# A full float32 product for probabilities times v, in place of three split ones

## The reference

```python
q = rmsnorm(ln(x) @ wq.T, q_norm_w); k = rmsnorm(ln(x) @ wk.T, k_norm_w)   # 16 heads of 128
v = ln(x) @ wv.T
q, k = apply_rope(q), apply_rope(k)
scores = 50 * tanh(q @ k.T * 128 ** -0.5 / 50)        # causal mask, then softmax
x = x + (softmax(scores) @ v) @ wo.T                  # stage 1, attention
x = x + wkv(w, u, ln(x), ctx)                         # stage 2, a recurrence over the 128 positions
x = x + moe(ln(x)) + shared_ffn(ln(x))                # stage 3, 16 experts, top 6, and a shared one
```

## Time and profile before

| | |
|---|---|
| timed runs | 2131.62 us median of 3, 2123.41 to 2139.04 |
| the profiled execution: span from first to last instruction | 2047.4 us |
| its own device time | not given; the median of the timed runs is 84.2 us over the span |
| PE matmul busy | 1982.2 us, 97% of the span |
| PE weight load, DVE, ACT, POOL busy | 87%, 54%, 45%, 50% |
| mean granted clock of PE | 0.990 |

### The profile page before, as it was taken

The page is one execution under the profiler, slowest core; times in us unless marked ns, Lnnn a source line. Parts: engine busy times, 40 slices in busy tenths (PEclk is TensorE's granted clock), DMA queues, the critical chain, the costliest instruction groups (busy, mean ns, idle before and its releaser), DMA issues.

```text
span 2047.4 us, 40563 instructions
## 1 busy us (share of the span) xinstructions
PE 1982.2 (97%) x12012; PEld 1790.4 (87%) x12013; DVE 1112.9 (54%) x2413; ACT 917.8 (45%) x2119; POOL 1013.5 (50%) x1076
## 2 busy tenths in 40 slices
PE   6999999999999999999989999999999999999998
PEld 5788888888888888888878898899999999999997
DVE  4776666666677776777667555333333333333332
ACT  4555555554566666656555312233333333323332
POOL 5444444442344444544556206676733333588885
PEclk8999999999999999999989999999999999999999
DMA  8677777778877878788534238666633443499899
GB/s 321 199 240 257 254 255 253 256 254 279 295 256 282 322 252 304 279 280 288 199 117 167 93 104 284 210 217 216 229 122 121 123 129 123 143 214 218 193 213 242
DMA packets 188986, 450.47 MB, mean 220 GB/s; under 512 B 21696, under 2 KB 21952, under 8 KB 188864
## 3 DMA queue, kind: packets, MB, share of 16 engines
q1 hardware_dynamic: 135392, 338.68, 49.1%
q0 software_dynamic: 21504, 51.13, 10.6%
q10 hardware_dynamic: 31968, 59.12, 9.0%
HBM read 275.36 MB, written 173.48 MB: 219 GB/s over the span
## 4 chain that ended last, share of the span: by engine, by line
PE 84%; DVE 4%; DMA 3%; ACT 3%; POOL 2%; issue 2%; SPq 1%; ACTq 0%; POOLq 0%; DVEq 0%
PE bank L1139 21%; PE bank L979 15%; PE bank L1149 12%; PE bank L1030 7%; PE bank L1004 7%; PE bank L165 6%; PE bank L582 4%; PE bank L1016 3%; PE bank L592 3%; PE bank L599 2%; PE bank L1051 2%; PE bank L1063 1%; DMA xT<-xT_att 1%; DMA raw<-in_weights 1%; PE bank L1041 1%
## 5 line engine op out<-in xcount | busy, mean ns | idle before, releaser
L1139 PE MATMUL bank<-w_hi,xT 128*128 x1776 | 473.7, 329 | 2.3 <-DVE xT L1734 2.1
L979 PE MATMUL bank<-w_hi,xT 128*128 128x512 f32 x1024 | 356.3, 409 | 6.2 <-issue 3.3
L609 DVE TENSOR_TENSOR hT<-bank,hT 128x384 fp32r<-128x384 f32 x143 | 79.7, 557 | 472.5 <-ACT hT L606 472.5
L1139 PEld LDWEIGHTS bank<-w_hi,xT 128*128 128x128 f32 x1776 | 315.7, 188 | 10.3 <-issue 5.1
L1422 POOL TENSOR_TENSOR rr<-rr,expo 128x4 f32<-128x4 f32 x128 | 129.0, 1008 | 365.8 <-DVE rr L1620 365.8
L1139 PE MATMUL bank<-w_lo,xT 128*128 x888 | 286.3, 322 | 0.0
L979 PEld LDWEIGHTS bank<-w_hi,xT 128*128 128x128 f32 x1024 | 196.5, 192 | 47.3 <-issue 6.6
L1149 PE MATMUL bank<-w_hi,hT 128*128 x666 | 230.3, 400 | 2.4 <-DVE hT L609 2.4
L606 ACT ACTIVATE hT<-bank 128x384 fp32r<-128x384 f32 x143 | 70.2, 491 | 330.5 <-PE bank L599 319.5
L1004 PE MATMUL bank<-w_hi,xT 128*128 128x256 f32 x1024 | 214.1, 292 | 0.0
L979 PE MATMUL bank<-w_lo,xT 128*128 128x512 f32 x512 | 203.5, 398 | 0.0
(11 more groups left out here) (248 smaller groups left out, 4467.2 us busy)
## 6 DMA issues: line engine op xcount, KB each, us to landing
xT<-xT_att SPq DMA_DIRECT2D x126, 512.0 KB, 5.2
w_hi<-w_split SPq DMA_DIRECT2D x64, 512.0 KB, 6.7
w_lo<-w_split SPq DMA_DIRECT2D x64, 512.0 KB, 7.7
xg<-blank SPq DMA_DIRECT2D x111, 264.0 KB, 4.8
yg<-blank SPq DMA_DIRECT2D x111, 256.0 KB, 5.8
raw<-in_weights SPq DMA_DIRECT2D x82, 272.0 KB, 3.1
w_split<-w_hi SPq DMA_DIRECT2D x64, 272.0 KB, 3.4
w_split<-w_lo SPq DMA_DIRECT2D x64, 272.0 KB, 3.7
```

Of the source, the lines that this page charges most:

```text
L609: dve.tensor_tensor(hT[:, 1, :], src[:, 0:IP], hT[:, 0, :].bitcast(F32), ALU.subtract).then_inc(hT_lo, 1)
L979: last = pe.matmul(bank[par][:, :], xT[:, par, a, c * P:(c + 1) * P], w_hl[w][:, fw, c * 512:(c + 1) * 512], start=n == 0, stop=n == 11)
L1139: last = pe.matmul(out_[:, 0:I], xT[:, par, a, c * P:(c + 1) * P], flat(w_hl[w])[:, bass.ds(at + (c * 2 * I + half_ * I), I)], start=n == ...
```

## The change

The three split products of each head become one float32 product. For this pT and vE become float32 tiles without a low part; pT gets two buffers, by step. ACT's copy to pT and DVE's two subtractions go; POOL's mask multiply writes pT. POOL waits for pv_done of two steps back before it writes. ACT's write of vE stays (float32 now, v_out), and PE waits for it alone. The memsets of the two extra columns fall from twelve to four, all ones, so the last column, unused, is one and not zero. The scores stay split.

```diff
-        vE = sb_early("vE", [P, 4, 2, HG, 130], F32R)
-        pT = sb_early("pT", [P, 2, HG, T], F32R)
+        vE = sb_early("vE", [P, 4, HG, 130])
+        pT = sb_early("pT", [P, 2, HG, T])
@@ PE, step
-                        wait(pe, v_hi, s)
-                        wait(pe, v_lo, s)
+                        wait(pe, v_out, s)
...
-                        pe.wait_ge(p_hi, s - 1)
-                        pe.wait_ge(p_lo, s - 1)
-                        pe.wait_ge(v_hi, s - 1)
-                        pe.wait_ge(v_lo, s - 1)
+                        pe.wait_ge(p_done, s - 1)
+                        pe.wait_ge(v_out, s - 1)
                         for h in range(HG):
-                            for n, (a, w) in enumerate(TERMS):
-                                last = pe.matmul(O_[:, h * 130:(h + 1) * 130], pT[:, a, h, :],
-                                                 vE[:, (at4 - 2) % 4, w, h, :], start=n == 0, stop=n == 2)
+                            last = pe.matmul(O_[:, h * 130:(h + 1) * 130], pT[:, 1 - par, h, :],
+                                             vE[:, (at4 - 2) % 4, h, :], start=True, stop=True)
...
-                            pe.wait_ge(v_hi, s + 1)
-                            pe.wait_ge(v_lo, s + 1)
+                            pe.wait_ge(v_out, s + 1)
@@ ACT, step
-                        act.activation(vE[:, at4, 0, :, 0:DH], heads(V_[:, 0:256]), ACT.Copy).then_inc(v_hi, 1)
+                        act.activation(vE[:, at4, :, 0:DH], heads(V_[:, 0:256]), ACT.Copy).then_inc(v_out, 1)
...
-                        wait(act, p_lo, s - 1)
+                        wait(act, p_done, s - 1)
                         act.activation(ex, th, ACT.Exp, scale=CAP).then_inc(ex_done, 1)
...
-                    if mid:
-                        act.wait_ge(mask_done, s)
-
-                        act.activation(pT[:, 0, :, :], heads(ex), ACT.Copy).then_inc(p_hi, 1)
@@ POOL
                 for par in range(4):
-                    pool.memset(vE[:, par, 0, :, 128:129].bitcast(F32), 1.0).then_inc(consts, 1)
-                    pool.memset(vE[:, par, 0, :, 129:130].bitcast(F32), 0.0).then_inc(consts, 1)
-                    pool.memset(vE[:, par, 1, :, 128:130].bitcast(F32), 0.0).then_inc(consts, 1)
-                pool.wait_ge(consts, 19)
+                    pool.memset(vE[:, par, :, 128:130], 1.0).then_inc(consts, 1)
+                pool.wait_ge(consts, 11)
...
                         pool.wait_ge(ex_done, s)
-                        pool.tensor_tensor(heads(ex), heads(ex), mask[:, :, :], ALU.mult).then_inc(mask_done, 1)
+                        wait(pool, pv_done, s - 2)
+                        pool.tensor_tensor(pT[:, par, :, :], heads(ex), mask[:, :, :], ALU.mult).then_inc(p_done, 1)
@@ DVE, step
-                        dve.wait_ge(v_hi, s + 1)
-                        dve.tensor_tensor(vE[:, at4, 1, :, 0:DH], heads(V_[:, 0:256]),
-                                          vE[:, at4, 0, :, 0:DH].bitcast(F32), ALU.subtract).then_inc(v_lo, 1)
...
-                    if mid:
-                        dve.wait_ge(p_hi, s)
-                        dve.tensor_tensor(pT[:, 1, :, :], heads(ex), pT[:, 0, :, :].bitcast(F32),
-                                          ALU.subtract).then_inc(p_lo, 1)
```

More of the change, by code:

```diff
@@ L186, in build @@
         NSIDE = 6
-        (qk_done, s_done, ot_done, v_done, wo_done, pv_done, t_done, sq_done, th_done, ex_done, oT_hi, p_hi,
-         v_hi, qkT_hi, k_out, ss_done, oT_lo, p_lo, v_lo, acc_done, rden_done, on_done, qkT_lo,
-         mask_done, ms_done, pw_done, rms_done, rot_done) = (sem(n) for n in (
+        (qk_done, s_done, ot_done, v_done, wo_done, pv_done, t_done, sq_done, th_done, ex_done, oT_hi,
+         v_out, qkT_hi, k_out, ss_done, oT_lo, acc_done, rden_done, on_done, qkT_lo,
+         p_done, ms_done, pw_done, rms_done, rot_done) = (sem(n) for n in (
              "qk_done", "s_done", "ot_done", "v_done", "wo_done", "pv_done", "t_done", "sq_done", "th_done",
-             "ex_done", "oT_hi", "p_hi", "v_hi", "qkT_hi", "k_out", "ss_done", "oT_lo", "p_lo", "v_lo",
-             "acc_done", "rden_done", "on_done", "qkT_lo", "mask_done", "ms_done", "pw_done",
+             "ex_done", "oT_hi", "v_out", "qkT_hi", "k_out", "ss_done", "oT_lo",
+             "acc_done", "rden_done", "on_done", "qkT_lo", "p_done", "ms_done", "pw_done",
              "rms_done", "rot_done"))
@@ L986, in step @@
                         pe.wait_ge(loA, READY)
-                        pe.wait_ge(consts, 19)
+                        pe.wait_ge(consts, 11)
                     if mid:
```

## The result

The changed kernel takes 2100.77 us (median of four runs, 2099.22 to 2103.36) against 2132.35 of the kernel before (2123.41 to 2139.04, four runs): a ratio of 0.9846, with a 95% interval of 0.9816 to 0.9875. The forecast was 2102.

A forecast was written before the change was run, and what follows sets the result against it. PE, busy in 97% of the span, was taken as the bound. 27 + 3.6 + 0.4 - 1.4 = 29.6 us off the 2047.4 span gives 2018, plus a constant 84.2 makes 2102 us; range 2086 to 2131.

The forecast's parts named there:

- The slots: Attention's edited product on PE: four load-and-matmul pairs in 0.46 us a step in place of 0.67, 27 us gained over 128 steps.
- Rival 1: Edited product: each of four passes carries its own load, 0.90 us a step, +29 us, 2157; chance 0.09 with its milder form.
- its milder form: Edited product: a pair stays near 0.215 us with a full 128-column load, +24 - 4 us, 2152; within Rival 1's 0.09.
- The feeders: ACT's copy and DVE's two differences before the product: removal worth nothing by itself, as PE wasn't waiting in the ordinary step.
- won't become the bound: Chain from ACT's square of new q and k to norms, rot and weight splitting speeds up about as much as PE's step (0.21).
- The late waits: PE's waits for p: 3.6 us gained in attention's last steps, and 0.4 us more in three early steps bound by DVE.
- What is given back: PE's waits before L979: xT landing within 0.2 us of its use in some 7 of 64 steps loses 1.4 us.
- rival 2: Transfers bound attention's second half: 64 late steps give nothing, 16 us gained, 2115; sign: idle before L979 beyond 15 us; chance 0.13.
- The handover: Stretch from 1040 to 1150 us, with 14 us of PE idle: attention's gain should pass through what follows unchanged.
- rival 3: Between 1040 and 1150 us the last 64 steps' gain (13 us) becomes waiting, 2115; sign: 25 us of idle; chance 0.07.
- The constant: Timed median 2131.62 us lies 84.2 above the profiled span of 2047.4; taken as constant and added to the new span.
- 1150 to the end as long as before: Sign to look for in the changed kernel's profile: the part behind attention and handover keeps its length.

The follow-up runs named there:

- the 66 columns: Changed kernel with only the last 66 of each head's 130 columns in the product (half of v's columns left out): 2090.62 us.
- the 256 columns: Changed kernel with the v projection as four float32 products of 256 columns in place of twelve split ones, low parts left out: 2122.91 us.
- feeders_alone: Changed kernel with three split product calls a head put back, all of the high parts; copy and subtractions stay removed: 2112.83 us, 0.9925 of the kernel before.
- before_again: Kernel before, unedited, timed and profiled once more: 2126.43 us, ratio 1.0001.
- after_again: Changed kernel, unedited, timed again in more rounds beside the kernel before: 2091.32 us, ratio 0.9834.
- keep_p_chain: Changed kernel with ACT's copy and DVE's subtraction for p put back as unread work that is waited for, without v's subtraction: 2038.69 us, 0.9951 of the kernel before.
- keep_v_low: Changed kernel with only DVE's subtraction for v put back as unread work that PE waits for: 2019.3 us, 0.9859 of the kernel before.
- pe_alone: Changed kernel with ACT's copy and DVE's two subtractions kept as unread work that is waited for: 2115.86 us, 0.9949 of the kernel before.
- before_no_scatter: Kernel before without the last four of six rounds of POOL's indirect stores for the experts: 2047.18 us, 0.9995 of the kernel before.
- after_no_scatter: Changed kernel without the last four of six rounds of POOL's indirect stores for the experts: 2009.12 us, 0.9809 of the kernel before.
- scores_full: Changed kernel with the scores also as one float32 product a head, without DVE's qkT subtraction and wide-scores sum: 2060.05 us, 0.9672 of the kernel before.

## Why the prediction was right, and where it wasn't

**The slots: right.** The working wanted 0.46 a step and 27 us; the slots have 0.452 and sum to 28.8 less. "It is the number of loads that counts" is borne out by the 66 columns, which cost the same, and its other side by the 256 columns, which cost more than twelve split slots. Rival 1 and its milder form, a pair of 0.215, are out: four loads take 0.45 and not 0.86 to 0.90. (The trace of before has eight float32 calls outside attention, not six; the two of L743, with four records, show two pairs each as well.) The Trainium skill, FP8 and Floating Point Precision, section TensorE Precision Notes, has a float32 product as four passes; with two loads and half the column rate a call, the rows fit that at 256 columns, and at 130 and 66 the passes are hidden behind the loads.

**The feeders: wrong, the one step that failed.** "PE was not waiting there in the ordinary step, so this is worth nothing by itself" is true of the ordinary step (7.31 in feeders_alone) and was carried over to all others but six. Each alone, the feeders are worth 19 us of attention and the slots 12; together they are worth 33 to 40 (three pairs of profiles: before_again with after and with after_again, and the two without the scatter). I had looked for the chain's price as idle time of PE in front of the product, 7.9 us. Taken out alone, it gains 4.6 us up to step 63, 9.8 in the next 64 and 4.3 at the end: in the steps with new weights (0.2 us each), in the early odd steps (0.33 each, as the forecast's 0.34) and beside the recurrence. In the one step shown above the copy stood in front of other work on ACT, and its price came back to PE at the scores and the transposes; keep_p_chain and keep_v_low show that in the other kinds of step too it is the p chain that costs.

Counted behind the slots the same gain divides otherwise. Up to step 63 the three pairs gain 13.2 to 14.7 us, where 61 products at 0.22 make 13.5; in the next 64 steps 14.9 to 22.8, where 64 make 14.2; behind them 4.7 to 4.8, where three make 0.7. pe_alone, with the chain kept, gains 5.1, 6.3 and 0.7. So for the most part the feeders' going does no more than let the slots count in full, which the forecast's 27 us took for granted. What comes on top lies in step 64 (9.0 to 9.4 us before, 7.32 after), step 126 and the end. With the slots at 28.8 and the change of each pair's idle time at L979 (below) allowed for, 8 to 12 us are left for the feeders, where 4.0 were forecast. The statement that the chain "won't become the bound" holds for the changed kernel and shows how near it was: with it kept, PE's shorter steps hit it at 7.25.

**The late waits: right in kind.** 4.0 us were forecast for the last steps and three early ones. Waits before the product fell from 7.9 to 2.0. That rest is one wait for POOL in step 126, the one of 2.73 that was to lose 0.9. The step went from 11.72 in the first profile to 9.58, but it is loose (13.03 in before_again, 11.14 in after_again). The steadier part is the end of attention, behind step 127: it is 4.7 to 4.8 us shorter in the three pairs (3.1 against the first profile), where the forecast had 2.7 for its two waits.

**What is given back: not settled.** 1.4 us was the sum for xT landing late. Idle time before L979 went from 6.2 to 10.1 us between the first two profiles, and from 6.4 in before_again to 9.6 in after_again. But on the third chip it fell, from 8.2 in before_no_scatter to 7.4 in after_no_scatter, so a loss of 3 to 4 us is in two pairs and none in the third. No profile comes near the 15 us that rival 2 wanted, and its condition fails outright: the two common lengths of a step in the second half, 7.55 and 7.96 us in before_again, are 7.33 and 7.76 in the changed kernel, so these steps do get their slots' gain.

**The handover: right.** Between 1040 and 1150 PE now idles 110 - 102.87 = 7.1 us, from this row:

```profile
1040.00:1150.00 110.00, 102.87 (x602) 94.50 (x601) 69.97 (x110) 49.12 (x84) 45.46 (x37) 0.98 0.40 130
```

against 13.6 before. That window has moved by the gain, so the whole stage is the better measure: it has 31 us of idle in the profile after and 32 in before_again, and rival 3 is out.

**The constant: wrong, without effect.** The 84.2 us were no time around the span (that is 1.8 to 2.2 us in every run with both numbers) but a difference between two executions of the same kernel. "1150 to the end as long as before" fails against the first profile (761.3 and 827.8 us for the experts) and holds against before_again to 9 us, and in after_again to 1. Since both kernels pay it alike on the same chip, adding it as a constant came out right, by luck and not by reading.

So the number came out (29.6 us forecast, 31.6 measured in the first comparison) with the feeders' term 4 to 8 us too small. The measured gain is 31.6, 36.2 and 38.1 us in three comparisons; that the first came within 2 us is in part luck, since attention alone gained 33 to 40 us in the pairs of profiles, and beside before_again the first profile lost 12 of its 37.5 again in stages that no line of the change touches.

## What to carry to other kernels

Price a float32 product against a three-term split by slots: two load-and-matmul pairs against three, each as long as the longer of its load (0.112 us here for 128 columns) and its moving columns (0.84 ns each in float32; the split ones no more than about 0.46 by their 0.118 for 256). By these numbers it pays up to an estimated 3 x 0.112 / (2 x 0.00084) = 200 columns, between 128 and 130, where it won, and 256, where it lost. The place counts as well: in front of the two transposes, four such pairs of 128 columns took 0.56 us and not 0.45, and six split ones 0.81 and not 0.67, with the same winner. Price the feeding work that an edit removes by taking it out alone: idle time in front of the edited line is only a small part of what a late chain costs, since it shows up at other lines and in long records.

## What the runs showed of the hardware

The course of the same program behind attention depends on the chip, or on the execution: handover and experts take 240 to 243 and 759 to 762 us in the first profile of before and in all four on the third chip, 261 to 265 and 818 to 828 in the others (but for scores_full's handover, 246). In these longer ones PE's progress reaches the other engines late while POOL issues its stores. From the timeline of the changed kernel:

```profile
1361.90 0.49 PE L599 MATMUL bank<-ident,hid 128*128 128x128 f32 x3
...
1364.41 0.32 PE L1134 MATMUL bank<-w_hi,xT 128*128 x1
...
1375.33 0.96 POOL L1468 DMA_INDIRECT xg<-xnB,a  x1 [0.30 <-issue]
1377.69 0.49 ACT L606 ACTIVATE hT<-bank 128x384 fp32r<-128x384 f32 x1 [15.67 <-remote]
1379.02 0.79 PE L1144 MATMUL bank<-w_hi,hT 128*128 x1 [14.29 <-issue]
```

ACT's copy L606 takes the bank that L599's transposes had filled by 1362.4, and starts 15 us later, when POOL's round is over; PE, with nothing left after 1364.7, idles 14.29 us. The windows around it, the granted clock being the third number from the end:

```profile
1355.00:1364.50 9.50, 9.50 (x61) 8.83 (x59) 2.26 (x4) 2.24 (x5) 7.52 (x8) 1.00 0.84 284
1364.50:1379.00 14.50, 0.23 (x2) 0.00 (x0) 0.56 (x1) 0.84 (x2) 9.14 (x11) 0.63 0.53 205
1379.00:1383.00 4.00, 3.98 (x12) 3.28 (x13) 1.70 (x3) 1.04 (x3) 0.00 (x0) 0.63 0.25 68
1383.00:1387.00 4.00, 4.00 (x29) 3.97 (x28) 0.56 (x1) 1.47 (x4) 0.00 (x0) 1.00 0.17 66
```

The clock falls to its half level (1.2 GHz) in the idle time and is back at 2.4 GHz by 1383, so each such stop costs somewhat more than its own length: PE has 12 matmul records in the 4 us at 0.63 and 29 in the next 4. In before_again and after_again 68 and 64 of PE's 1661 semaphore updates arrive more than 1 us late, by up to 22 us; in the first profile of before none does. The same holds throughout: 62 to 74 late ones in each profile with the longer experts' stage, none or one in each on the third chip. That the stores cause it wasn't tested on a chip that shows it, and stays open.
